# Moving the x projection of a four-direction selective scan into the in_proj and convolution stage

## Chip, cores and metric

The kernel runs on one core of one Trainium2 chip, as one launch. The metric is the device time of that launch in microseconds, as the median of several runs.

## What is computed

Four layers, one after the other, each on 4 images of 64 x 64 pixels with 192 channels. Cut to what matters here, one layer of the first three is:

```python
xn  = group_norm(x)                               # 192 channels
xc, z = split(xn @ in_proj.T)                     # 384 + 384 channels
u   = silu(depthwise_conv3x3(xc))                 # layers 1, 2, 3; layer 0 has u = xc
for k in range(4):                                # four scan directions over the 4096 pixels
    uk = order_k(u)                               # rows, columns, rows backwards, columns backwards
    dts, B, C = split(x_proj[k] @ uk)             # R + 16 + 16 rows; R = 12, 12, 96 in layers 0, 1, 2
    dt  = softplus(dt_w[k] @ dts + dt_bias[k])    # 384 channels
    h   = exp(dt * A) * h + dt * uk * B           # a scan over 4096 steps, 16 states a channel
    y  += back_k(sum_n(h * C) + D * uk)
x = x + out_proj(layer_norm(y) * gate(z))
```

Layer 3 has no scan: its convolution goes straight to the output stage. Everything is float32.

## The kernel before

The program loops over the images, and in each over the layers; a layer is up to three stages with a barrier of all engines behind each: `norm_conv`, `scan` (layers 0 to 2), `out_proj`. The 4096 pixels are cut into NCH = 8 chunks of T = 512, and the 384 inner channels into NDB = 3 blocks of 128 partitions. Orders of instructions inside a stage are written out by hand, per engine, and held together by semaphores.

**norm_conv** (L205 to L426). TensorE projects chunk by chunk (L403, 6 matmuls a chunk, two PSUM halves of 3 banks in turn), ScalarE normalises the next chunk's input (L356), VectorE copies the result out of PSUM: to `u` in layer 0, into the padded image `pad` otherwise (L305). Only when all 8 chunks are in `pad` does the convolution begin, as a second loop: 4 taps of 9 are matmuls with a diagonal matrix (L420), 5 taps are VectorE operations (L333, 15 a chunk), and ScalarE applies SiLU (L379). The last engine to finish ends the stage.

**scan** (L429 to L880). It opens with a preamble that projects direction k = 0 for all 8 chunks (L544 on TensorE, L755 on ScalarE, stores of `xd` and `b` to device memory on SyncE's queue, L507 and L456) and then loads the first chunk's inputs. The main part runs over 4 directions x 8 chunks x 3 blocks, 96 units a layer. A unit has 8 steps g of two states each. Per step TensorE multiplies dt*u by B through block-diagonal matrices (`inputs`, L583) and transposes weighted states to sum them (`sums`, L597), ScalarE makes the decays (L725) and keeps the last state (L714), VectorE scans (L828), GpSimd weighs with C (L868). Once a unit `make_dt` runs (L806, L811) on VectorE, at step g = 3 of the unit before, so the starts of L806 mark the units. In directions k = 0 to 2 the block d = 1 of each chunk also carries `project_x` for direction k + 1 of the same chunk (L544, one matmul at each of g = 5, 6, 7, into the bank that softplus uses):

```python
if d == 1 and g >= PE_XD and k + 1 < K:
    if g == PE_XD:
        pe.wait_ge(dt_made, unit(this, NDB - 1) + 1)
    project_x(k + 1, n, Z_BANK, g - PE_XD)
```

It reads `u` in the order of direction k + 1 (`in_order`, L167), which for odd directions is a column walk with a step of 64 floats. ScalarE takes the result out of PSUM (L781) and issues two stores (L785, L456). Direction k = 3 has nothing left to project.

The B rows of a chunk go from `b_dram` into a zeroed matrix in device memory, 4 bytes at a time, 4096 pieces to a DMA and two DMAs a chunk, on ScalarE's queue (`spread`, L708); from there they are loaded as `diag` (L487). The C rows are loaded broadcast to 128 partitions, four DMAs a chunk (`load_c`, L499), each of 4 rows that lie together in device memory.

Of the kernel before, what the change touches and what calls it, by code (L numbers as in the profile page):

```python
# [19 lines left out]
F32 = mybir.dt.float32  # L20
# [4 lines left out]
P = 128  # L25
IMAGES, H, W = 4, 64, 64
L = H * W
# [13 lines left out]
PE_LAG, PE_Z, PE_SKIP, PE_Y, PE_XD, PE_TR = 3, 1, 4, 5, 5, 6  # L41
ACT_B, ACT_XD, ACT_IN, ACT_LOG, ACT_YT, ACT_Y, ACT_TR = 4, 0, 2, 3, 3, 6, 7
# [4 lines left out]
PE_TAPS = 4  # L47
GN_EPS = 1e-5
LN_EPS = (1e-6, 1e-6, 1e-5, 1e-5)
RANK = (12, 12, 96)  # L50
MAX_LOG = 83.0
# [10 lines left out]
B_SCAN = (2 * RING + 4 + 2 + 1 + 2 + 1 + 3 + 1 + 1) * T  # L62
B_OUT = NCB * 2 * DI + NDB * DM + 2 * NDB * T + 2 * T + NCB * NCH * 6
# [9 lines left out]
def build(nc, x_in, ident_in, group_in, ones_in, w_in, w_out, w_xp, w_dt, vecs, out):  # L73
# [3 lines left out]
    with ctx:  # L77
# [18 lines left out]
        xp_w = sb("xp_w", [P, 2, NDB, P])  # L96
# [19 lines left out]
        xd_out = regB[:, o:o + T]; o += T  # L116
# [4 lines left out]
        xd_sb2 = dt  # L121
# [6 lines left out]
        tap_w = regB[:, o:o + PE_TAPS * NDB * P].rearrange("p (k d j) -> p k d j", k=PE_TAPS, d=NDB)  # L128
        xn = spare[0:CB, 0:2 * NCB * T].rearrange("p (q c t) -> p q c t", q=2, c=NCB)
        cv = spare[:, 2 * NCB * T:(2 * NCB + 2 * NDB) * T].rearrange("p (q d t) -> p q d t", q=2, d=NDB)  # L130
# [7 lines left out]
        x_stats = regB[0:CB, o:o + NCB * NCH * 6].rearrange("p (c n s) -> p c n s", c=NCB, n=NCH)  # L138
# [4 lines left out]
        xd_dram = [nc.dram_tensor(f"xd_{l}", (K, NCH, 1 + RANK[l] + 2 * NS, T), F32).ap() for l in range(3)]  # L143
# [4 lines left out]
        sems = [ctx.enter_context(nc.semaphore(f"s{i}")) for i in range(36)]  # L148
        all_sems = range(sems[0].num, sems[-1].num + 1)
        assert [s.num for s in sems] == list(all_sems)  # L150
# [51 lines left out]

        def norm_conv(l, b):
# [3 lines left out]
             cv_used, act_own, dve_own, a_made) = sems[:24]  # L207
            weights = 32 if last else 64

            XN_FREE, PAD_FREE = 2, 2  # L210
            CV_FREE = 2 * NDB
            DT_TAPS = TAPS - PE_TAPS
            STEP_FREE = CV_FREE * DT_TAPS

            with nc.Block(no_gpsimd_drain=True) as block:
                @block.sync
                def _(sp):
# [6 lines left out]
                    sp.dma_start(out_w, w_out[l]).then_inc(w_ready, 16)  # L224
                    if not last:
                        M = RANK[l] + 2 * NS
                        sp.dma_start(xp_w[:, :, :, 0:M], w_xp[l][:, 0:2]).then_inc(w_ready, 16)
                        sp.dma_start(dt_w[0:RANK[l] + 1], w_dt[l][:, 0:2]).then_inc(w_ready, 16)
                    if l in (1, 2):

                        sp.dma_start(x_dram, xT).then_inc(x_saved, 16)
                        sp.wait_ge(x_saved, 16)
# [4 lines left out]
                    sp.wait_ge(w_ready, weights)  # L237

                @block.gpsimd
                def _(pool):  # L240
                    if conv:
                        v = pad[:].rearrange("p d (h w) -> p d h w", w=PW)
# [3 lines left out]
                        nc.gpsimd.memset(v[:, :, 1:PW - 1, PW - 1], 0.0).then_inc(border, 1)  # L246

                @block.vector
                def _(dve):
                    dve.sem_inc(pad_made, PAD_FREE)  # L250
                    if conv:
                        dve.sem_inc(cv_step, STEP_FREE)

                    if l == 0:
                        for h, loaded in enumerate((x_half0, x_half1)):
                            dve.wait_ge(loaded, 16)
                            with dve.Fori(0, NCH // 2) as j:
                                chunk_stats(j + h * (NCH // 2), stats_made)
# [32 lines left out]

                    v = pad[:].rearrange("p d (h w) -> p d h w", w=PW)
                    if conv:
                        dve.wait_ge(border, 4)
                    with dve.Fori(0, NCH // 2) as j:
                        for q in range(2):
                            c = j * 2 + q
                            dve.wait_ge(in_mm, XN_FREE + c + 1)
# [937 lines left out]
```

## Time and profile before

| | |
|---|---|
| median of 3 runs | 30196.06 us (30186.81 to 30205.66) |
| the profiled execution: its own time, its span | 30209.58 us, 30207.7 us |
| PE, DVE, POOL, ACT busy, share of the span | 94%, 85%, 79%, 63% |
| TensorE clock granted, mean | 0.97 |
| device memory moved | 2545.53 MB read, 123.73 MB written, 88 GB/s |
| scan stages | 12 (3 layers x 4 images), 18432 scans, 1152 units |

The profile is of one execution. Shares are means over stages that differ much, so the stages are read one by one below. A layer's stages are told apart by the lines that open them: ScalarE's table load L340 opens norm_conv, L744 opens scan, L1001 opens out_proj.

### The profile page before, as it was taken

To read this page: it belongs to the slowest core of one execution; us is meant where nothing else is said; L and a number is where in the kernel's file an instruction comes from. 1 tells how busy PE (TensorE), PEld (TensorE's weight loads), DVE (VectorE), ACT (ScalarE), POOL (GpSimd) and SP (SyncE) were. 2 spreads that over 40 slices of the span, in tenths; PEclk is the share of its full clock that TensorE was granted. 3 is DMA by queue.
4 is the path that set the end of the run, shared out by engine and by line. 5 is a ranking of instruction groups with operands and counts; after the bars stand their busy time and mean duration, and the time that the engine had idled before them with its cause. 6 is when DMAs were issued, how large, how long until landed. Compare 5 with 4: busy or idle time off the path is not lost. (4 is left out here: it accounts for less than half of the span.)

```text
span 30207.7 us, 612992 instructions
## 1 busy us (share of the span) xinstructions
PE 28498.1 (94%) x244800; PEld 20286.3 (67%) x244800; DVE 25621.6 (85%) x23482; ACT 19104.5 (63%) x38088; POOL 23845.1 (79%) x10772
## 2 busy tenths in 40 slices
PE   9998998998999899899899989989989998998998
PEld 6775775774677577577467757757746775775774
DVE  7987996996798799699679879969968987996996
ACT  5665774774566577477466657747746665774774
POOL 7986995994798699599479869959947986995994
PEclk9999999999999999999999999999999999999999
DMA  3332332331333233233133323323313332332331
GB/s 100 100 95 71 102 103 67 106 108 43 97 101 94 71 102 102 69 105 109 42 97 100 94 71 102 103 69 105 109 43 97 102 91 74 102 101 69 106 107 43
DMA packets 3579914, 2695.33 MB, mean 89 GB/s; under 512 B 3269236, under 2 KB 3273548, under 8 KB 3323832
## 3 DMA queue, kind: packets, MB, share of 16 engines
q1 hardware_dynamic: 353272, 2592.36, 23.8%
q10 hardware_dynamic: 3223872, 64.57, 6.5%
q8 instruction: 1918, 31.42, 0.4%
q14 instruction: 852, 6.98, 0.1%
HBM read 2545.53 MB, written 123.73 MB: 88 GB/s over the span
## 5 line engine op out<-in xcount | busy, mean ns | idle before, releaser
L868 POOL TENSOR_TENSOR regB<-regB,regA 128x1024 f32<-128x1024 f32 x9216 | 21558.4, 2369 | 1760.6 <-ACT carry L714 1743.2
L828 DVE TENSOR_TENSOR_SCAN regB<-regB,carry,ps 128x512 f32<-128x512 f32 x16128 | 19217.5, 1259 | 1197.4 <-PE ps L583 1177.4
L725 ACT ACTIVATE regB<-regB,a_neg 128x512 f32<-128x512 f32 x18432 | 12225.6, 712 | 0.6
L583 PEld LDWEIGHTS ps<-regA,regB 64*128 64x128 f32 x147456 | 8992.5, 188 | 4164.4 <-issue 3185.4
L583 PE MATMUL ps<-regA,regB 64*128 64x128 f32 x147456 | 10739.4, 285 | 77.5 <-DVE regB L828 59.0
L597 PE MATMUL ps<-ident,regB 128*128 128x128 f32 x73728 | 10083.6, 280 | 184.3 <-POOL regB L868 125.2
L597 PEld LDWEIGHTS ps<-ident,regB 128*128 128x128 f32 x73728 | 7906.5, 141 | 1349.6 <-POOL regB L868 317.6
L714 ACT ACTIVATE carry<-regB 128x2 f32<-128x2 f32 x9216 | 1900.2, 206 | 5949.7 <-DVE regB L828 5358.8
L858 POOL TENSOR_TENSOR regB<-regB,u 128x512 f32<-128x512 f32 x1152 | 1630.5, 1415 | 2142.0 <-DVE regB L811 2142.0
L828 DVE TENSOR_TENSOR_SCAN regB<-regB,ps 128x512 f32<-128x512 f32 x2304 | 2624.5, 1201 | 375.1 <-PE ps L583 341.4
L544 PE MATMUL ps<-u,xp_w 128*44 128x512 f32 (+3 forms) x2304 | 1678.7, 834 | 158.4 <-ACT L744 114.0
L1139 POOL TENSOR_TENSOR regB<-regB 128x512 f32<-128x512 f32 x128 | 187.0, 1461 | 2006.8 <-ACT regB L1026 2006.6
L614 PE MATMUL ps<-pad,ident 128*128 128x512 f32 x1728 | 1376.4, 883 | 8.2 <-ACT regB L734 8.2
L558 PE MATMUL ps<-regB,dt_w 13*128 13x512 f32 (+1 forms) x2304 | 1268.6, 631 | 78.7 <-DMA regB<-xd 78.7
L806 DVE SCALAR_TENSOR_TENSOR ps<-regB,ps 128x512 f32<-128x512 f32 x1152 | 776.9, 674 | 477.5 <-ACT regB L684 477.5
L692 ACT ACTIVATE regB<-ps 128x512 f32<-128x512 f32 x1152 | 671.4, 583 | 746.6 <-PE ps L565 746.3
L420 PE MATMUL ps<-pad,regB 128*128 x2304 | 1012.9, 602 | 30.1 <-DVE pad L305 30.1
L740 ACT ACTIVATE pad<-ps 128x512 f32<-128x512 f32 x1152 | 943.9, 819 | 38.9 <-PE ps L620 38.9
L927 PE MATMUL ps<-regA,regB 96*128 96x512 f32 x1536 | 702.7, 621 | 272.1 <-ACT regA L983 272.1
L565 PEld LDWEIGHTS ps<-ident,regB 128*128 128x128 f32 x4608 | 537.8, 143 | 474.8 <-issue 391.9
L420 PEld LDWEIGHTS ps<-pad,regB 128*128 128x128 f32 x2304 | 442.5, 193 | 600.4 <-issue 600.4
L675 ACT ACTIVATE regB<-ps 128x512 f32<-128x512 f32 x1152 | 681.2, 591 | 240.1 <-PE ps L558 223.1
(81 smaller groups left out, 14465.4 us busy)
## 6 DMA issues: line engine op xcount, KB each, us to landing
regA<-xd SPq DMA_DIRECT2D x1536, 1024.0 KB, 4.7
regA<-eye SPq DMA_DIRECT2D x384, 2048.0 KB, 7.7
regA<-x_in SPq DMA_DIRECT2D x16, 1536.0 KB, 14.4
x_keep<-regA SPq DMA_DIRECT2D x8, 3072.0 KB, 18.8
regA<-x_keep SPq DMA_DIRECT2D x16, 1536.0 KB, 15.9
regB<-xd SPq DMA_DIRECT2D x128, 192.0 KB
xd<-regB ACTq DMA_DIRECT2D x96, 256.0 KB
xd<-regB ACTq DMA_DIRECT2D x192, 88.0 KB
```

What stands on the lines that cost most here:

```text
L420: last_mm = nc.tensor.matmul(ps[:, 3 * q + d, :].rearrange("p (r w) -> p r w", w=W), tap_w[:, tap, d, :], v[:, d, bass.ds(c * RW + tap // ...
L544: mm = nc.tensor.matmul(as_chunk(ps[0:M, bank, :], k), xp_w[:, k % 2, d, 0:M], in_order(u, k, d, n), start=d == 0, stop=d == NDB - 1)
L558: nc.tensor.matmul(ps[:, Z_BANK, :], dt_w[0:R + 1, k % 2, d * P:(d + 1) * P], dts[0:R + 1], start=True, stop=True).then_inc(z_mm, 1)
L583: mm = nc.tensor.matmul(b.rearrange("p (t s) -> p s t", s=2), dtuT[at, up, q, :], diag[at, cp, q, g], start=True, stop=True)
L597: mm = nc.tensor.matmul(ps[:, Y_BANK + up, at], ring[:, g % RING, s, at], ident[:], start=g == 0 and s == 0 and q == 0, stop=g == PAIRS - ...
L614: nc.tensor.matmul(as_chunk(ps[:, Y_BANK + up, :], k), w, in_order(src, k, d, n), start=True, stop=False)
L714: nc.scalar.activation(carry[:, d, 2 * g:2 * g + 2], ring[:, g % RING, :, T - 1 if c[0] < 2 else 0], ACT.Copy).then_inc(carried, 1)
L725: nc.scalar.activation(decays[:, g % 2, s], dt[:, up, :], ACT.Exp, scale=a_neg[:, c[0], d, 2 * g + s:2 * g + s + 1]).then_inc(a_made, 1)
L740: nc.scalar.activation(in_order(y_acc, k, d, n), as_chunk(ps[:, Y_BANK + up, :], k), ACT.Copy).then_inc(y_kept, 1)
L828: nc.vector.tensor_tensor_scan(ring[:, g % RING, s, way], decays[:, g % 2, s, way], b[:, s, way], 0.0 if begun else carry[:, d, at:at + 1] ...
L858: nc.gpsimd.tensor_tensor(dtu.rearrange("p (q i r) -> p i q r", i=ROWS, q=QS), dt[:, up, :].rearrange("p (i q r) -> p i q r", i=ROWS, q=QS ...
L868: nc.gpsimd.tensor_tensor(ring[:, g % RING], ring[:, g % RING], c_all[:, g], ALU.mult).then_inc(g_made, 1)
```

## The change

`norm_conv` becomes one pipeline over chunks, written out without hardware loops, that also makes the x projection of all four directions; `scan` loses both the preamble and `project_x`.

- The projection is made in plain pixel order from the chunk of `u` just made. In layers 0 and 1 two directions share one matmul of 2 x 44 output rows (`PASSES`), so a chunk has 2 passes of 3 matmuls; in layer 2 (128 rows a direction) 4 passes of 3.
- Device memory holds `xd` as whole rows of 4096 pixels in the order of the direction's walk (`xd_dram`, now K x rows x L). The even directions (0, 2) are stored by SyncE as pieces of 512 pixels. For the odd directions (1, 3) ScalarE writes its PSUM copy transposed to (w, h) order, 8 pixels of a column together, and issues the stores itself: every piece is 8 floats, 32 bytes. Nothing in `norm_conv` waits for the last of these; `scan` waits for them before direction 1.
- With a transposed copy, B and C rows of chunk n in a backwards direction are those of chunk 7 - n (`place`).
- The number of taps on TensorE is 0, 2, 1, 3 in layers 0 to 3 (before 4 everywhere); VectorE has the other 7, 8 and 6 in layers 1 to 3.
- `pad` is filled by ScalarE instead of VectorE (`fill_pad`), `out_w` is no longer loaded in `norm_conv` of layers 0 to 2, and the store of x to `x_keep` is waited for late.
- The first chunk's `dts`, `diag` and C rows are loaded at the end of `norm_conv`, by SyncE behind `store_even(6)`.
- C rows now lie 16 KB apart, so a load of 4 rows reads 2 KB pieces where it read 8 KB.

```diff
-PE_TAPS = 4
+PE_TAPS = (0, 2, 1, 3)
+PASSES = (((0, 2), (1, 3)), ((0, 2), (1, 3)), ((0,), (2,), (1,), (3,)))
...
-        xd_dram = [nc.dram_tensor(f"xd_{l}", (K, NCH, 1 + RANK[l] + 2 * NS, T), F32).ap() for l in range(3)]
+        xd_dram = [nc.dram_tensor(f"xd_{l}", (K, 1 + RANK[l] + 2 * NS, L), F32).ap() for l in range(3)]
...
+                    store_even(0)
+                    store_even(1)
+                    sp.wait_ge(even_stored[0], EVEN)
+                    sp.wait_ge(ones_set, 1)
+                    sp.dma_start(dts[0:RANK[l]], dts_rows(l, 0, 0)).then_inc(dts_loaded, 16)
+                    spread_rows(sp, l, 0, 0, 0, spread_b)
+                    for c in range(2, NCH):
+                        store_even(c)
+                        if c == NCH - 2:
...
+                            sp.dma_start(diag[:, 0].rearrange("p q g t -> p (q g t)"),
+                                         eye_dram[0, 0:P * EYE].rearrange("(p x) -> p x", p=P)).then_inc(diag_loaded, 16)
+                            sp.wait_ge(in_mm, NCH)
+                            for h in range(PAIRS // 2):
+                                sp.dma_start(c_all[:, 2 * h:2 * h + 2], c_rows(l, 0, 0, h).partition_broadcast(P)
+                                             ).then_inc(c_loaded, 16)
...
+                    def keep_x(c):
...
+                        for i, ks in enumerate(passes):
+                            n, rows = c * NP + i, len(ks) * M
+                            odd = i >= NP // 2
+                            act.wait_ge(xd_mm, n + 1)
...
+                            if odd:
+                                wait(act, odd_stored[c % 2], c // 2 * odd_each(l))
+                            else:
+                                wait(act, even_stored[c % 2], c // 2 * EVEN)
+                            dst, src = staged(i, c)[0:rows], ps[0:rows, 6 + n % 2, :]
+                            if odd:
+                                dst = dst.rearrange("p (w h) -> p h w", h=RW)
+                                src = src.rearrange("p (h w) -> p h w", w=W)
+                            nc.scalar.activation(dst, src, ACT.Copy).then_inc(xd_copied, 1)
...
+                                for part in odd_parts(l):
+                                    act.dma_start(to[part], rows[part]).then_inc(odd_stored[c % 2], 16)
+                                to = b_dram[l][k].rearrange("c (a n r) -> n (c a) r", n=NS, r=H)[:, :, c * RW:(c + 1) * RW]
+                                act.dma_start(to, rows[RANK[l]:RANK[l] + NS]).then_inc(odd_stored[c % 2], 16)
...
+                    for c in range(NCH + 1):
+                        if c:
+                            silu(c - 1)
+                        if c + 4 < NCH:
+                            normalise(c + 4)
+                        if c + 3 < NCH:
+                            fill_pad(c + 3)
+                        if c:
+                            keep_x(c - 1)
...
+                    for c in range(NCH + 1):
+                        if c + 1 < NCH:
+                            taps(c + 1)
+                        if c + 3 < NCH:
+                            project_in(c + 3)
+                        if c:
+                            project_x(c - 1)
...
-                                if d == 1 and g >= PE_XD and k + 1 < K:
-
-                                    if g == PE_XD:
-                                        pe.wait_ge(dt_made, unit(this, NDB - 1) + 1)
-                                    project_x(k + 1, n, Z_BANK, g - PE_XD)
```

**TensorE in the scan**, block d = 1 of a chunk in direction 0, before (L583 is `inputs`, L597 `sums`, L620 `turn_y`, L565 `turn_dtu`, L544 `project_x`):

```order
L583 MATMUL ps<-regA,regB 128x2x64 x8
L597 MATMUL ps<-ident,regB 128x128 x8
L620 MATMUL ps<-ident,regB 128x128 x4
L544 MATMUL ps<-u,xp_w 44x512
L583 MATMUL ps<-regA,regB 128x2x64 x8
L597 MATMUL ps<-ident,regB 128x128 x8
L544 MATMUL ps<-u,xp_w 44x512
L565 MATMUL ps<-ident,regB 128x128 x4
L583 MATMUL ps<-regA,regB 128x2x64 x8
L597 MATMUL ps<-ident,regB 128x128 x8
L544 MATMUL ps<-u,xp_w 44x512
```

and the same place after (L711, L725, L748, L693 in that order of names):

```order
L711 MATMUL ps<-regA,regB 128x2x64 x8
L725 MATMUL ps<-ident,regB 128x128 x8
L748 MATMUL ps<-ident,regB 128x128 x4
L711 MATMUL ps<-regA,regB 128x2x64 x8
L725 MATMUL ps<-ident,regB 128x128 x8
L693 MATMUL ps<-ident,regB 128x128 x4
L711 MATMUL ps<-regA,regB 128x2x64 x8
L725 MATMUL ps<-ident,regB 128x128 x8
```

The three projection matmuls are gone and nothing stands in their place.

**ScalarE in norm_conv of layer 2**, one chunk in the middle, after (L437 `silu`, L423 `normalise`, L429 `fill_pad`, L456 the copies of `keep_x`, L465 and L467 its stores; the last numbers of a DMA's shape are pieces and floats a piece):

```order
L437 ACTIVATE u<-regB,vec 128x512 x3
L423 ACTIVATE regA<-regA,gn_bias,gn_rstd 96x512 x2
L429 ACTIVATE pad<-ps 128x3x8x64
L456 ACTIVATE regB<-ps 128x512 x2
L456 ACTIVATE xd_odd<-ps 128x8x64 x2
L465 DMA xd<-xd_odd 3072x1x8 x2
L465 DMA xd<-xd_odd 1024x1x8
L467 DMA b<-xd_odd 16x64x8
L465 DMA xd<-xd_odd 3072x1x8 x2
L465 DMA xd<-xd_odd 1024x1x8
L467 DMA b<-xd_odd 16x64x8
```

Before, this loop held L379 alone; now each chunk issues 8 DMAs of 16384 pieces in all from this engine's queue (in layers 0 and 1 there are 6 DMAs of 5632 pieces).

## Rows read from the trace of the kernel before

**Rows 1.** The page, busy time by engine over the span.
```profile
PE 28498.1 (94%) x244800; PEld 20286.3 (67%) x244800; DVE 25621.6 (85%) x23482; ACT 19104.5 (63%) x38088; POOL 23845.1 (79%) x10772
```

**Rows 2.** Busy time by stretch: directions 0 to 2 and 3, layers 1 and 2.
```profile
core 0: us, PE busy (x) PEld busy (x) DVE busy (x) ACT busy (x) POOL busy (x), PEclk, DMA share, GB/s
10114.10:11684.60 1570.50, 1552.39 (x14722) 1160.92 (x14723) 1441.69 (x1289) 1085.38 (x2243) 1427.61 (x643) 1.00 0.35 101
11684.60:12156.90 472.30, 471.56 (x4695) 369.23 (x4694) 463.23 (x416) 351.05 (x713) 463.57 (x208) 1.00 0.35 104
12557.90:14120.50 1562.60, 1530.35 (x14721) 1172.46 (x14722) 1442.41 (x1288) 1084.09 (x2242) 1427.72 (x643) 0.99 0.36 107
14120.50:14589.20 468.70, 467.40 (x4695) 368.69 (x4694) 463.25 (x416) 349.90 (x713) 463.04 (x208) 1.00 0.36 107
```

**Rows 3.** Waits of DVE in one scan of layer 1 (total us, times, longest).
```profile
DVE regB L828 <- PE ps L583: 134.5, 160, 5.3
```

**Rows 4.** Timeline of DVE, `make_dt` alone: start, us; directions 0, then 1.
```profile
10547.10 0.68 DVE L806 SCALAR_TENSOR_TENSOR ps<-regB,ps 128x512 f32<-128x512 f32 x1
10572.42 0.67 DVE L806 SCALAR_TENSOR_TENSOR ps<-regB,ps 128x512 f32<-128x512 f32 x1
10592.49 0.67 DVE L806 SCALAR_TENSOR_TENSOR ps<-regB,ps 128x512 f32<-128x512 f32 x1
...
10742.96 0.68 DVE L806 SCALAR_TENSOR_TENSOR ps<-regB,ps 128x512 f32<-128x512 f32 x1
10766.62 0.67 DVE L806 SCALAR_TENSOR_TENSOR ps<-regB,ps 128x512 f32<-128x512 f32 x1
10787.18 0.68 DVE L806 SCALAR_TENSOR_TENSOR ps<-regB,ps 128x512 f32<-128x512 f32 x1
```

**Rows 5.** Timeline of PE in that scan, direction 0, `project_x` and its neighbour.
```profile
10554.87 1.89 PE L544 MATMUL ps<-u,xp_w 128*44 128x512 f32 x2
10556.69 0.66 PE L565 MATMUL ps<-ident,regB 128*128 128x128 f32 x4
```

**Rows 6.** Busy time from the start of norm_conv to the first scan, layers 0 to 3 (layer 3: to out_proj).
```profile
7563.60:7684.60 121.00, 74.67 (x174) 29.34 (x176) 27.47 (x39) 26.19 (x41) 1.26 (x1) 0.77 0.33 83
9926.80:10120.90 194.10, 158.44 (x366) 66.27 (x368) 98.14 (x143) 47.47 (x78) 2.44 (x5) 0.89 0.17 52
12364.20:12564.60 200.40, 162.58 (x366) 71.29 (x368) 98.03 (x142) 47.50 (x78) 2.41 (x5) 0.88 0.21 62
14797.10:14944.70 147.60, 129.50 (x292) 56.74 (x292) 96.11 (x138) 35.12 (x57) 1.10 (x4) 0.93 0.03 7
```

**Rows 7.** Timeline of PE: first in_proj matmuls of layer 0; taps of layer 1 (two records are one matmul).
```profile
7591.50 18.79 PE L403 MATMUL ps<-regA,regB 96*128 96x512 f32 x38 [2.67 <-ACT regA L356]
...
9994.58 21.62 PE L420 MATMUL ps<-pad,regB 128*128 x50
```

**Rows 8.** L333 alone over the convolution of layer 1: us, DVE busy (x), PEclk, DMA share, GB/s.
```profile
9984.20:10071.80 87.60, 80.26 (x120) 0.97 0.00 0
```

**Rows 9.** Timeline of the start of scan, layer 1.
```profile
10073.58 1.28 ACT L744 ACT_TABLE_LOAD   x1 [0.91 <-PEq L426]
...
10114.15 0.70 DVE L806 SCALAR_TENSOR_TENSOR ps<-regB,ps 128x512 f32<-128x512 f32 x1 [39.90 <-ACT regB L684]
...
10120.89 1.22 DVE L828 TENSOR_TENSOR_SCAN regB<-regB,ps 128x512 f32<-128x512 f32 x1 [5.32 <-PE ps L583]
```

**Rows 10.** Costs of ScalarE's pieces, by form (busy us, mean ns, idle before).
```profile
L379 ACT ACTIVATE u<-regA,vec 128x512 f32 x288 | 196.7, 724 | 1004.9 <-DVE regA L333 1004.9
...
L995 ACT ACTIVATE u<-ps 128x1536 f32<-128x1536 f32 x48 | 69.7, 1452 | 179.5 <-PE ps L927 179.5
```

**Rows 11.** Timeline of ACT and its sequencer in the scan: the two DMAs of `spread`.
```profile
10524.37 0.54 ACTq L708 DMA_DIRECT2D eye<-b  x1
...
10524.94 3.15 ACTq L708 DMA_DIRECT2D eye<-b  x1
```

**Rows 12.** The page, DMA queue of ScalarE (packets, MB, share of 16 engines); issues with KB each, us to landing.
```profile
q10 hardware_dynamic: 3223872, 64.57, 6.5%
...
regA<-xd SPq DMA_DIRECT2D x1536, 1024.0 KB, 4.7
regA<-eye SPq DMA_DIRECT2D x384, 2048.0 KB, 7.7
...
eye<-b ACTq DMA_DIRECT2D x768, 16.0 KB, 11.2
```

More of the change, by code:

```diff
@@ L256, in _ @@
                             dve.wait_ge(loaded, 16)
-                            with dve.Fori(0, NCH // 2) as j:
+                            for j in range(NCH // 2):
                                 chunk_stats(j + h * (NCH // 2), stats_made)
@@ L363, in _ @@
                     if not conv:
+                        normalise(2)
+                        for c in range(NCH):
+                            if c + 3 < NCH:
+                                normalise(c + 3)
+                            keep_x(c)
                         return
@@ L366, in _ @@
                     act.wait_ge(w_ready, weights)
-                    for tap in range(PE_TAPS):
+                    for tap in range(PT):
                         for d in range(NDB):
@@ new lines, in _ @@
+                    fill_pad(0)
+                    normalise(2)
+                    fill_pad(1)
+                    normalise(3)
+                    fill_pad(2)
+                    for c in range(NCH + 1):
[7 more added lines that the diff above has]
+                            keep_x(c - 1)
@@ new lines, in taps @@
+                    def taps(c):
+                        pe.wait_ge(pad_made, min(c + 2, NCH))
+                        for d in range(NDB):
+                            if c:
+                                pe.wait_ge(cv_step, step_of(c - 1, 0, d))
+                            for tap in range(PT):
+                                mm = nc.tensor.matmul(
+                                    ps[:, d, :].rearrange("p (r w) -> p r w", w=W), tap_w[:, tap, d, :],
+                                    v[:, d, c * RW + tap // 3:c * RW + tap // 3 + RW, tap % 3:tap % 3 + W],
+                                    start=tap == 0, stop=tap == PT - 1)
+                            mm.then_inc(cv_mm, 1)
@@ new lines, in project_x @@
+                    def project_x(c):
+                        if last:
+                            return
+                        ready_u(pe, c)
+                        for i, ks in enumerate(passes):
+                            n, rows = c * NP + i, len(ks) * M
+                            wait(pe, xd_copied, n - 1)
+                            for d in range(NDB):
+                                w = (i * NDB + d) * rows
+                                mm = nc.tensor.matmul(ps[0:rows, 6 + n % 2, :], xp_w[:, w:w + rows],
+                                                      u[:, d, c * T:(c + 1) * T], start=d == 0, stop=d == NDB - 1)
+                            mm.then_inc(xd_mm, 1)
@@ L407, in _ @@
+                    project_in(1)
+                    if not last:
+                        pe.wait_ge(xw_loaded, 16)
                     if not conv:
+                        for c in range(NCH):
+                            if c + 2 < NCH:
+                                project_in(c + 2)
+                            project_x(c)
                         return
-                    v = pad[:].rearrange("p d (h w) -> p d h w", w=PW)
-                    pe.wait_ge(tap_made, PE_TAPS * NDB)
+                    pe.wait_ge(tap_made, PT * NDB)
```

355 lines of the change are left out of this document (171 added, 184 removed).

## Prediction

> **What bounds the kernel now.** I read the busy shares first [rows 1]. TensorE is busy 94% of the span and VectorE 85%, so either could set the pace, and a mean over stages cannot say which. The next view is busy time by stretch, with the borders put on the directions of one scan [rows 2]. Directions 0 to 2 of layer 1 take 1570.5 us and direction 3 takes 472.3 us, from the first `make_dt` of a direction to that of the next, and for direction 3 to its last one. That is 72 units at 21.81 us against 23 intervals at 20.53 us. The only work that direction 3 lacks is `project_x` with its copy and stores, so the kernel holds its own comparison: a unit with nothing to project is 1.28 us shorter on average. In the same stretches PE is busy 1552 of 1570 us and 471.6 of 472.3 us. VectorE waits for TensorE's L583 134.5 us in one scan [rows 3]. The scan is bound by TensorE, with VectorE and GpSimd just behind: in direction 3 they are busy 463 us each of 472.
>
> The timeline of `make_dt` shows where it goes [rows 4]. In direction 0 the interval that holds `project_x` lasts 10572.42 - 10547.10 = 25.32 us, and the one behind it 20.07 us. In direction 1 they are 23.66 and 20.56 us. So one chunk's projection costs 5.25 us where it reads columns (for directions 1 and 3) and 3.10 us where it reads rows (for direction 2). The PE timeline agrees with the first: one L544 matmul to its successor is 1.82 us [rows 5], three are 5.5. A tap matmul, read in rows, takes 21.62 / 25 = 0.865 us [rows 7].
>
> Then the stages between the scans [rows 6]: from the start of norm_conv to the first scan 121.0, 194.1 and 200.4 us in layers 0, 1, 2, and 147.6 us for layer 3 up to out_proj. VectorE is busy in half of that, since the convolution only starts when in_proj has ended and the scan's preamble comes behind both.
>
> **What leaves the scan.** `project_x`, 24 chunks a scan. In layers 0 and 1: 16 x 5.25 + 8 x 3.10 = 108.8 us, if the freed interval falls to that of its neighbour [rows 4]. The other way to count is to give every unit direction 3's interval: 1570.5 - 72 x 20.53 = 92 us [rows 2]. I take the first, because even directions show 20.07 us where TensorE has nothing extra, and keep the second as the low end. For layer 2 I take the same count by blocks: 1562.6 - 72 x 20.38 = 95 us. Per image 2 x 108.8 + 95 = 313 us (low end 279). VectorE is late next, and `spread` still holds ScalarE once a chunk. The C loads now read 2 KB pieces. They land 4.7 us after issue now [rows 12] and are wanted about six steps of 2.5 us later, so I cost them at nothing; that cover of some 10 us would have to be used up.
>
> **The preamble.** From scan's table load to the first `make_dt` is 40.6 us and from there to the first scan 6.7 us [rows 9]. The first shrinks to table load, three small scalings and four softplus steps, about 5.4 us by the same timeline. So 12 us stay of 47.
>
> **The norm_conv stages.** Their length now comes from the slowest engine of one pipeline.
>
> Layer 0: TensorE starts 27.9 us in [rows 6, 7] and has 8 x (6 + 6) matmuls: 96 x 0.865 = 83 us, up from 42. Behind it hang the loads of `diag` and C, issued some 5 us before TensorE ends; alone they take 7.7 + 4 x 4.7 = 26.5 us in a row [rows 12], overlapped less. I take 15 us exposed (ends 8 and 21). With a barrier: 127.5 + 12 = 139.6 us against 121.0, so **+19**.
>
> Layer 1: start-up about 22 us (two projected chunks, 10.4; two pad copies of 1.45 [rows 10]; first taps). Then per chunk TensorE has 18 matmuls, 15.6 us, and VectorE 21 tap operations at 87.6 / 120 = 0.73 us [rows 8], 15.3 us: 8 x 15.6 = 125. Tail: last SiLU 0.7, last x projection 5.2, copies, store issues and barrier 6. Sum 159 + 12 = 171 against 194.1: **-23**.
>
> Layer 3: 24 + 144 x 0.73 + 2.5 = 131.6 against 147.6: **-16**.
>
> Layer 2 turns on a cost that the trace shows only from afar. Its TensorE needs 21 matmuls a chunk, 18.2 us, and VectorE 17.5 us. But ScalarE's queue must also take 16384 pieces of 32 bytes per chunk. The nearest rows are the two `spread` DMAs of 4096 pieces of 4 bytes: the second one's issue holds ScalarE's sequencer for 3.15 us [rows 11], and what ScalarE has next stands behind it. They land 11.2 us after issue [rows 12]. The low end per piece is the busy time of the DMA engines: 6.5% of 30207 us on 16 engines over 3.22 million packets is 9.7 ns an engine, 0.61 ns a piece. The high end is one DMA alone, 11.2 us / 4096 = 2.7 ns. I take the pair, 11.2 / 8192 = 1.37 ns, since a long row of DMAs is most like a pair. Then a chunk's stores take 22.4 us, more than the 18.2 of TensorE, and with ScalarE held in their issue, `silu`, `normalise` and `fill_pad` of later chunks queue behind: the stage runs at the pace of the stores. First batch at 52 us, eight of 22.4, less 7.5 still in flight when ScalarE is let go, barrier and 12: 238 against 200.4, **+37**. At the low end the stage is TensorE's, 22 + 145 + 26 + 12 = 206, or +6. In layers 0 and 1 a chunk has 5632 pieces, 7.7 us, below the 10.4 and 15.6 us of TensorE: hidden, so long as a piece stays under 1.8 ns in layer 0.
>
> The trace shows 4-byte pieces leaving an engine every 9.7 ns [rows 12]. The Trainium skill's page "DMA: Bandwidth & Descriptors", section Specifications, says that transfers under 512 B make the DMA engine read, modify and write. If that doubled the engine's 9.7 ns it would be 1.2 ns a piece and 29,000 us in all, so rule and row part only if the penalty is several times larger, which is the fourth case below.
>
> **Sum.** Per image -313 + 19 - 23 + 37 - 16 = -296 us; four images -1184 us. On the profiled execution, 30209.6 us, that gives 29,025; the median of the runs is 13.5 us lower, so 29,010 us.
>
> **Other ways it could go.** (a) The stores cost 0.6 to 1.1 ns a piece: layer 2 costs +6, the sum is -328 an image, time 28,880. For it: 256 pieces an engine need only 2.5 us of its time. Against it: ScalarE visibly stands in L708.
> (b) The gain is smaller: scan intervals fall only to direction 3's 20.53 us and a piece costs 2 ns, so layer 2 is +120 and layer 0 +21: -279 + 21 - 23 + 120 - 16 = -177 an image, 29,490 us; with one of the two alone about 29,200 to 29,350. At 2.7 ns it would be 29,900.
> (c) The stores flood: each odd piece, written with a step of 256 bytes, is so dear that ScalarE's queue sets all three stages. At r ns a piece the three take, against now, 131 r - 142, 45 r - 143 and 45 r - 69 us; with -16 and -313 the sum is 221 r - 683 us an image. It decides from r = 3.1 ns, or 50 ns an engine; at 4 ns the time is 31,000. For it: each piece is a partial write, and no row shows 32 bytes to a strided place. Against it: L708 writes smaller ones to places as scattered at 1.37 ns.
> (d) The change does not do what it says: VectorE is the real bound, `project_x` was covered, and the scan stays at 2043 us. Then only the stages move, +17 an image, 30,265. The difference of 25.32 to 20.07 us in neighbouring units speaks against it [rows 4].
>
> **Chances.** Forecast 0.55, (a) 0.22, (b) 0.15, (c) 0.05, (d) 0.03. Within 0.2% (60 us, about what a measurement of this kernel can tell) has hardly a case of its own: 0.02, out of the edges of (b) and (d). Slower 0.06, faster 0.92. The range is 28,800 to 29,450: below, (a) with somewhat more won at the stages' tails; above, (b) without its worst corner.
>
> **What would show it.** Right: no interval between two `make_dt` over 21 us in steady chunks, even directions near 20.1, scans of 1930 to 1950 us from first to last `make_dt`; 12 us from scan's table load to the first scan; norm_conv of layer 2 with ScalarE's sequencer in L465 most of the time and chunks of about 22 us, layer 1's at 15.6. Wrong: chunks of layer 2 at 18 us or over 30; intervals near 20.5 in even directions; VectorE waiting for C loads at the start of chunks.

## Result and the profile after

The change made the kernel slower: 32007.41 us (median of 4 runs, 31997.39 to 32021.70) against 30191.44 us (4 runs, 30181.60 to 30205.66), a ratio of 1.060 with a 95% interval of 1.058 to 1.062. The forecast was 29,010 us with a range of 28,800 to 29,450. The profiled execution has a span of 31995.7 us.

From the page of the kernel after: busy time by engine, two of the costliest groups with the idle time ahead of them, DMA queues, and DMA issues with the median time to landing.

```profile
PE 27893.6 (87%) x242880; PEld 20718.7 (65%) x242880; DVE 25798.2 (81%) x23950; ACT 19104.5 (60%) x37984; POOL 23811.1 (74%) x10784
...
q1 hardware_dynamic: 1049336, 2606.52, 36.9%
q10 hardware_dynamic: 3953792, 40.59, 7.5%
...
L953 POOL TENSOR_TENSOR regB<-regB,regA 128x1024 f32<-128x1024 f32 x9216 | 21519.6, 2376 | 2908.7 <-ACT carry L820 2900.0
L914 DVE TENSOR_TENSOR_SCAN regB<-regB,carry,ps 128x512 f32<-128x512 f32 x16128 | 19186.7, 1258 | 2259.0 <-ACT regB L831 1528.1
...
regA<-xd SPq DMA_DIRECT2D x1536, 1024.0 KB, 11.1
regA<-eye SPq DMA_DIRECT2D x384, 2048.0 KB, 7.8
```

No engine is fuller than before [rows 1]: all four lose share, so the added time is waiting. Both large groups now wait for ScalarE. For GpSimd that is an old wait that has grown, for VectorE a new one; the same two groups on the page of the kernel before:

```profile
L868 POOL TENSOR_TENSOR regB<-regB,regA 128x1024 f32<-128x1024 f32 x9216 | 21558.4, 2369 | 1760.6 <-ACT carry L714 1743.2
L828 DVE TENSOR_TENSOR_SCAN regB<-regB,carry,ps 128x512 f32<-128x512 f32 x16128 | 19217.5, 1259 | 1197.4 <-PE ps L583 1177.4
```

And the C loads (`regA<-xd`) land 11.1 us after issue (the median) where they took 4.7 [rows 12], while the `diag` load beside them is nearly unchanged (7.8 against 7.7). Of queue q1 the 1,049,336 packets take 36.9% of the span. These loads overlap one another, so the rate of one can't be had by dividing 1 MB by its time to landing: over the four loads of one chunk 143 GB/s are moved, with the DMA engines busy for 0.85 of the time.

```profile
10882.60:10912.20 29.60, 26.61 (x274) 21.39 (x274) 25.53 (x24) 16.32 (x35) 22.22 (x11) 1.00 0.85 143
```

Busy time by stretch, the columns of [rows 2]: from norm_conv's start to the first scan in layers 0, 1, 2 (layer 3: to out_proj), then directions 0 to 2 and direction 3 of layer 1.

```profile
8000.30:8169.80 169.50, 93.32 (x220) 38.60 (x222) 27.05 (x37) 34.13 (x49) 1.79 (x2) 0.76 0.56 83
10482.30:10698.80 216.50, 144.14 (x318) 58.45 (x320) 115.33 (x182) 64.34 (x88) 2.87 (x6) 0.82 0.40 65
13035.80:13342.20 306.40, 174.64 (x366) 75.17 (x368) 131.20 (x205) 76.70 (x101) 2.91 (x6) 0.77 0.46 67
15688.20:15830.80 142.60, 110.52 (x244) 47.23 (x244) 98.45 (x154) 44.04 (x62) 1.18 (x4) 0.91 0.03 7
10692.00:12311.00 1619.00, 1484.15 (x14578) 1188.41 (x14579) 1437.99 (x1288) 1067.92 (x2218) 1423.89 (x643) 0.96 0.49 93
12311.00:12829.90 518.90, 488.95 (x4693) 384.64 (x4692) 464.41 (x415) 348.22 (x713) 463.92 (x208) 0.95 0.50 95
```

TensorE's busy time in directions 0 to 2 fell by 68 us, and the stretch still grew from 1570.5 to 1619.0. Direction 3, whose work the change does not touch, grew from 472.3 to 518.9 us. That alone says that something beside the removed projection was added to every chunk. TensorE's granted clock, 1.00 in both before, is 0.96 and 0.95 here, where it is idle between its matmuls for 134.9 of 1619.0 and 30.0 of 518.9 us.

All stages of image 1 (the second of four), in us; a scan is taken from its first `make_dt` to its last (the time from there to the first scan stays at 6.7), and the last rows are experiments told below:

| | to first scan, L0 / L1 / L2 | L3 | scans, L0 / L1 / L2 | kernel |
|---|---|---|---|---|
| before | 120.9 / 194.1 / 200.4 | 147.6 | 2044.0 / 2042.7 / 2031.3 | 30191 |
| forecast | 139.6 / 171 / 238 | 131.6 | 1935 / 1934 / 1936 | 29010 |
| after | 169.5 / 216.5 / 306.4 | 142.6 | 2112.5 / 2137.9 / 2147.5 | 32007 |
| e3, rows 18 KB apart | 147.2 / 202.6 / 285.6 | 142.7 | 1934.0 / 1938.5 / 1933.7 | 29443 |
| e5, and SyncE stores | 148.4 / 177.1 / 214.0 | 142.5 | 1939.0 / 1934.8 / 1937.9 | 29067 |
| e9, and late first loads | 131.8 / 165.4 / 198.8 | 142.2 | 1941.4 / 1939.6 / 1935.5 | 28901 |
| e10, after with late spread | 170.8 / 223.1 / 308.9 | 142.5 | 1984.7 / 1991.5 / 1967.3 | 30229 |
| e11, e9 with late spread | 133.0 / 165.6 / 199.3 | 144.2 | 1979.7 / 1981.3 / 1957.6 | 29347 |

Against the forecast, an image is 592 us longer in its scans and 155 us in its stages, 747 in all, and four such images make up 2,990 of the 2,997 us of the miss.

**Inside a chunk.** The timeline of VectorE, `make_dt` alone (start, us), direction 0 of layer 1:

```profile
10884.36 0.68 DVE L892 SCALAR_TENSOR_TENSOR ps<-regB,ps 128x512 f32<-128x512 f32 x1
10904.44 0.67 DVE L892 SCALAR_TENSOR_TENSOR ps<-regB,ps 128x512 f32<-128x512 f32 x1
10932.33 0.67 DVE L892 SCALAR_TENSOR_TENSOR ps<-regB,ps 128x512 f32<-128x512 f32 x1
10952.40 0.68 DVE L892 SCALAR_TENSOR_TENSOR ps<-regB,ps 128x512 f32<-128x512 f32 x1
```

Two intervals of three are 20.07 and 20.08 us, what a unit without projection took before [rows 4]; the third is 27.89. In it lie these rows of ScalarE (ACTq is its sequencer) and of SyncE's sequencer:

```profile
10902.23 0.52 ACTq L226 DMA_DIRECT2D eye<-b  x1
...
10902.78 9.65 ACTq L226 DMA_DIRECT2D eye<-b  x1
...
10912.48 0.20 ACT L820 ACTIVATE carry<-regB 128x2 f32<-128x2 f32 x1 [8.25 <-issue]
```

```profile
10882.63 15.95 SPq L646 DMA_DIRECT2D regA<-xd  x4
```

The four C loads are issued between 10882.6 and 10898.6, and the last of them, issued at 10898.22, takes 14.0 us and lands at 10912.2; `spread` (L226) comes at 10902, and its second DMA holds ScalarE's sequencer for 9.65 us where it took 3.15 [rows 11]. `keep_last` (L820) and the decays (L831) stand behind it. GpSimd waits for L820 as well:

```profile
10912.82 2.35 POOL L953 TENSOR_TENSOR regB<-regB,regA 128x1024 f32<-128x1024 f32 x1 [7.31 <-ACT carry L820]
```

Over the whole scan of layer 1, ScalarE's waits in the kernel after (us in total, times, longest): once a chunk, 31 times, it stands still for an issue, 245 us together.

```profile
ACT carry L820 <- issue: 244.9, 31, 10.8
```

The same row of the kernel before:

```profile
ACT carry L714 <- issue: 52.5, 28, 2.7
```

The difference, 192 us, is nearly the 204 by which that scan exceeds its forecast. SyncE's loads are not themselves awaited: no wait of GpSimd for `regA<-xd` stands among its waits there, and none of TensorE for `diag`.

The hold of 9.65 us ends at 10912.4, 0.3 us behind the landing of the last C load. It is so in nearly every chunk: over the 30 chunks of that scan it ends 0.9 us after the last landing (the median; four in five between 0.5 and 1.9 us). What holds the sequencer lasts as long as the C loads do.

**The steady part and the end of norm_conv.** ScalarE's timeline in layer 2, `silu` (L437) and the issue of the odd stores (L465, L467), in the steady part and at the end:

```profile
13198.82 1.95 ACT L437 ACTIVATE u<-regB,vec 128x512 f32<-128x512 f32 x3 [10.23 <-issue]
...
13212.88 4.84 ACTq L465 DMA_DIRECT2D xd<-xd_odd  x3
13217.76 0.67 ACTq L467 DMA_DIRECT2D b<-xd_odd  x1
13218.47 5.06 ACTq L465 DMA_DIRECT2D xd<-xd_odd  x3
13223.56 0.67 ACTq L467 DMA_DIRECT2D b<-xd_odd  x1
13224.28 1.95 ACT L437 ACTIVATE u<-regB,vec 128x512 f32<-128x512 f32 x3 [10.30 <-issue]
...
13266.11 31.17 ACTq L465 DMA_DIRECT2D xd<-xd_odd  x3
```

A chunk takes 25.5 to 26.9 us in this ring: `silu` 2, TensorE's x projection of that chunk 12 to 13.5 (10.5 in the first chunk, where the granted clock is 1.00; here it is 0.78 to 0.88), the last copy, which runs beside the first store's issue, 11.3 us of issue, and then the next `silu`, which stands behind the issue in ScalarE's queue. Near the end the same L465 takes 31.17 us instead of about 5: SyncE has just issued the next stage's `diag` and C loads,

```profile
13263.49 0.38 SPq L327 DMA_DIRECT2D regA<-eye  x1
13263.91 6.97 SPq L331 DMA_DIRECT2D regA<-xd  x4
```

and the last chunk's `silu`, projection and stores all wait. In layers 0 and 1 the pair of L465 in the same place holds ScalarE 26.65 and 20.83 us, against 1.5 to 2.3 us in other chunks.

### The profile page after: what moved, and what is told of

It reads as the page before. It is cut to its first block and busy times, and to the rows that moved or that the text cites. A ratio compares the mean times of both kernels' runs of the same rounds, so it can differ in the third digit from the quotient of the medians.

```text
span 31995.7 us, 601560 instructions
## 1 busy us (share of the span) xinstructions
PE 27893.6 (87%) x242880; PEld 20718.7 (65%) x242880; DVE 25798.2 (81%) x23950; ACT 19104.5 (60%) x37984; POOL 23811.1 (74%) x10784
## 3 DMA queue, kind: packets, MB, share of 16 engines
q1 hardware_dynamic: 1049336, 2606.52, 36.9%
## 5 line engine op out<-in xcount | busy, mean ns | idle before, releaser
L831 ACT ACTIVATE regB<-regB,a_neg 128x512 f32<-128x512 f32 x18432 | 12184.5, 710 | 0.6
L725 PE MATMUL ps<-ident,regB 128*128 128x128 f32 x73728 | 10406.8, 286 | 1844.3 <-POOL regB L953 1830.2
L711 PEld LDWEIGHTS ps<-regA,regB 64*128 64x128 f32 x147456 | 9212.7, 192 | 3602.0 <-issue 2917.1
L711 PE MATMUL ps<-regA,regB 64*128 64x128 f32 x147456 | 10974.3, 289 | 115.1 <-DVE regB L914 71.0
L725 PEld LDWEIGHTS ps<-ident,regB 128*128 128x128 f32 x73728 | 8174.6, 144 | 3019.3 <-POOL regB L953 1955.2
L820 ACT ACTIVATE carry<-regB 128x2 f32<-128x2 f32 x9216 | 1884.7, 204 | 8309.9 <-DVE regB L914 5405.3
L550 PE MATMUL ps<-u,regB 128*88 128x512 f32 (+1 forms) x1536 | 779.6, 667 | 620.9 <-ACT u L437 613.9
L414 DVE SCALAR_TENSOR_TENSOR regB<-pad,vec,regB 128x512 f32<-128x512 f32 x1728 | 1152.8, 745 | 0.0
L550 PEld LDWEIGHTS ps<-u,regB 128*88 128x88 f32 (+1 forms) x1536 | 297.4, 197 | 1094.9 <-ACT u L437 653.9
L693 PE MATMUL ps<-ident,regB 128*128 128x128 f32 x4608 | 862.7, 320 | 83.2 <-POOL regB L943 82.9
L804 ACT ACTIVATE regB<-ps 128x512 f32<-128x512 f32 x1152 | 671.9, 583 | 302.8 <-PE ps L693 302.7
L897 DVE TENSOR_TENSOR regB<-ps,regB 128x512 f32<-128x512 f32 x1152 | 796.8, 692 | 39.5
## 6 DMA issues: line engine op xcount, KB each, us to landing
regA<-xd SPq DMA_DIRECT2D x1536, 1024.0 KB, 11.1
```

What stands on the lines that cost most here:

```text
L414: nc.vector.scalar_tensor_tensor(dst, src, wt, part, ALU.mult, ALU.add).then_inc(cv_step, 1)
L550: mm = nc.tensor.matmul(ps[0:rows, 6 + n % 2, :], xp_w[:, w:w + rows], u[:, d, c * T:(c + 1) * T], start=d == 0, stop=d == NDB - 1)
L711: mm = nc.tensor.matmul(b.rearrange("p (t s) -> p s t", s=2), dtuT[at, up, q, :], diag[at, cp, q, g], start=True, stop=True)
L725: mm = nc.tensor.matmul(ps[:, Y_BANK + up, at], ring[:, g % RING, s, at], ident[:], start=g == 0 and s == 0 and q == 0, stop=g == PAIRS - ...
L820: nc.scalar.activation(carry[:, d, 2 * g:2 * g + 2], ring[:, g % RING, :, T - 1 if c[0] < 2 else 0], ACT.Copy).then_inc(carried, 1)
L831: nc.scalar.activation(decays[:, g % 2, s], dt[:, up, :], ACT.Exp, scale=a_neg[:, c[0], d, 2 * g + s:2 * g + s + 1]).then_inc(a_made, 1)
```

## Experiments

Each runs beside the kernel before on the same chip, which took 30272.62 us in the first group (e1 to e4), 30250.59 in the second (e5 to e8) and 30257.52 in the third (e9 to e11); with the change itself it took 30191.44. So a difference between runs of two groups can be some 80 us off, and where it is small the stage times in the table bear it out. Where no interval is given, the time is of one run.

**e1: the kernel before with rows 16 KB apart.** One line of layout and its reader; nothing is moved.

```diff
-        xd_dram = [nc.dram_tensor(f"xd_{l}", (K, NCH, 1 + RANK[l] + 2 * NS, T), F32).ap() for l in range(3)]
+        xd_dram = [nc.dram_tensor(f"xd_{l}", (K, 1 + RANK[l] + 2 * NS, L), F32).ap() for l in range(3)]
```

> The kernel before with one part of the change alone: xd in device memory as rows of 4096 pixels, so that the four C rows of a load are 2 KB pieces 16 KB apart instead of 8 KB in one piece. Theory A (the C loads are what stretches the scan: 2 KB pieces take the DMA engines 177 ns each, a load lands after 11 us instead of 4.7, and ScalarE's issue of the spread DMAs is held behind them): every chunk's first full unit grows by 6 to 8 us, a scan by 170 to 210 us, the kernel comes out near 32,300 to 32,700 us, with C loads landing after 10 to 11 us. Rival B (the stretch of the scan comes from something else in the changed kernel, such as where the small stores put the B rows): about 30,200 us, C loads at 4.7 us.

Measured: 32640.11 us, 2,367 more than before. Its page (C loads) and its ACT timeline:

```profile
regA<-xd SPq DMA_DIRECT2D x1536, 1024.0 KB, 10.9
```

```profile
10930.01 11.91 ACTq L708 DMA_DIRECT2D eye<-b  x1
```

The layout alone makes the slow loads, the long hold, and scans of 2224 to 2258 us. The miss of the forecast's scans, 4 x 592 = 2,368 us, is about as large.

**e2: the kernel before with pieces of 2 KB, rows 2,112 bytes apart.** It tells the size of the pieces from the distance of the rows.

```diff
-(K, NCH, 1 + RANK[l] + 2 * NS, T), F32).ap()
+(K, NCH, 1 + RANK[l] + 2 * NS, T + 16), F32).ap()[:, :, :, 0:T]
```

> The kernel before with its C rows kept close together but 64 bytes apart from each other, so that a load still reads 2 KB pieces, now at a pitch of 2112 bytes. If the size of the pieces is what costs (theory A1): as with rows 16 KB apart, 32,300 to 32,700 us, C loads landing after 10 to 11 us. If the pitch of 16 KB is what costs (A2): 30,200 us, loads at 4.7 to 5.5 us, a 2 KB piece at 90 ns.

Measured: 30254.49 us, within 0.1% of before; loads land after 5.6 us. Four times as many pieces are worth 0.9 us of landing and nothing of time. So the distance of the rows is the cause, and not the size of the pieces.

**e3: the change with rows 18 KB apart.** The same rows and pieces, 2 KB of padding behind each row.

```diff
-(K, 1 + RANK[l] + 2 * NS, L), F32).ap()
+(K, 1 + RANK[l] + 2 * NS, L + 512), F32).ap()[:, :, 0:L]
```

> The changed kernel with rows of xd 18 KB apart instead of 16 KB, nothing else. A1 (size): stays at 32,000 us. A2 (pitch of a power of two): the scan loses its stretch of 170 to 205 us, three scans and four images, and the ends of norm_conv some 20 us each: about 29,450 us.

Measured: 29443.39 us, 2,564 less than the change, 2.7% under the kernel before. Page and ACT timeline:

```profile
regA<-xd SPq DMA_DIRECT2D x1536, 1024.0 KB, 4.8
```

```profile
10905.46 3.41 ACTq L226 DMA_DIRECT2D eye<-b  x1
```

Over the four C loads of a chunk 158 GB/s are moved with the DMA engines busy for 0.51 of the time, against 143 at 0.85 in the change:

```profile
10885.00:10912.00 27.00, 26.93 (x280) 21.82 (x278) 26.54 (x26) 19.13 (x41) 26.10 (x13) 1.00 0.51 158
```

The scans are the forecast's within 5 us each. Of the 2,997 us of the miss this is 86%. The same 1,049,336 packets of queue q1 now take 25.6% of 29,442 us, 7,537 us for each of the 16 DMA engines against 11,806 in the change.

**e4: the change with the C rows of a chunk copied together in device memory** (one more small copy a chunk on SyncE, loads of 8 KB pieces from it).

```diff
+        c_dram = [nc.dram_tensor(f"c_{l}", (K, NCH, NS * T), F32).ap() for l in range(3)]
...
+            eng.dma_start(c_dram[l][k, n].rearrange("(m t) -> m t", t=T),
+                          xd_dram[l][k][o:o + NS, at * T:(at + 1) * T]).then_inc(sem, 16)
```

> The changed kernel with the 16 C rows of each chunk first copied inside device memory into 32 KB in one piece (one small DMA more a chunk, on SyncE's queue), and loaded from there in 8 KB pieces. Both A1 and A2: C loads land after about 4.7 us again, intervals of make_dt go to 20.1 and 20.6 us (the unit with the spread DMAs to 20.5), scans of 1930 to 1950 us instead of 2112 to 2145, ScalarE's issue of a spread DMA is held 3 us instead of 10, the 20 to 30 us for which it is held at the end of norm_conv shrink below 10: about 29,450 us. If the stretch has another cause: stays over 31,500 us.

Measured: 29553.28 us, scans 1938 to 1943, C loads 4.7 us. A second way to be rid of the stride gives the same scans; the stages are 7 us longer than in e3 in layer 0 and 9 in layer 2, with the copies in them.

**e6: the change with rows 16,448 bytes apart.** As e3 with `L + 16`.

> The changed kernel with rows of xd 64 bytes further apart (16448 bytes instead of 16384). If it is the exact power of two that makes the four rows of a load meet in the same part of the memory, and any offset spreads them: as with 18 KB, 29,450 us and C loads after 4.8 us. If the pieces must be kilobytes away from the same place: C loads stay at 8 to 11 us and the time above 31,000 us.

Measured: 31863.13 us; C loads 11.1 us, scans 2115 to 2141. Rows 64 bytes further apart load as slowly as in the change; 2 KB further apart they load quickly.

The Trainium skill's page "DMA: Bandwidth & Descriptors", section "Latency and other measured facts", says that large row distances at powers of two slow copies of 128 rows (207 GB/s at 512 KiB, 164 at 2 MiB, 103 at 4 MiB), that 4 KiB of padding restores the rate and 192 bytes don't. The runs agree in the shape of it: slow at 16 KB and 64 bytes beside it, quick with 2 KB of padding (e1, e6, e3; 10.9, 11.1 and 4.8 us to landing). They differ in the distance at which it begins: here it is 16 KB already, in a load of four rows read by 128 partitions.

**e10: the change as it is, with `spread` issued some 15 us later,** when the slow loads have landed. It tells the slow loads from the queue behind them.

```diff
-                                if d == 0 and after and g == ACT_B:
+                                if d == 1 and after and g == 2:
                                     spread(after, 1 - par)
```

> The change as it is, rows 16 KB apart, but ScalarE issues the spread of the next chunk's B rows in block d = 1, step 2, instead of block d = 0, step 4, some 15 us later, when the slow C loads have landed. Theory (ScalarE's queue is held behind the C loads, and that is what the scan loses): the hold of the second L226 falls from 9.65 us to about 3, C loads still land some 11 us after issue, and a scan takes 1940 to 1960 us from first to last make_dt instead of 2112 to 2148; total 29,650 to 29,850 us. Rival (the C rows themselves come late for GpSimd, or the traffic slows what runs beside it): a scan stays over 2050 us and the total over 31,000.

Measured: 30229.12 us (10 runs), ratio 0.999 (0.998 to 1.000). From its page, its ACT timeline, its waits of ACT and those of POOL in the scan of layer 1:

```profile
regA<-xd SPq DMA_DIRECT2D x1536, 1024.0 KB, 11.4
```

```profile
10923.57 2.81 ACTq L226 DMA_DIRECT2D eye<-b  x1
```

```profile
ACT carry L820 <- issue: 22.9, 7, 4.5
```

```profile
POOL regB L953 <- ACT carry L820: 100.9, 69, 6.7
POOL regB L953 <- DMA regA<-xd: 1.3, 2, 0.9
```

The loads are as slow as ever and GpSimd waits 1.3 us for them in a scan, but the long hold is gone and with it 1,778 us. The mechanism of the theory held. Its numbers did not: the scans, 1967 to 1992 us, all missed its 1940 to 1960, and the total missed its 29,650 to 29,850 by 379 us. e11 looks for the reason.

**e11: e9 with the same late spread,** to see what the new place costs by itself.

> The version with rows 18 KB apart, SyncE's odd stores and late first loads, and with the spread in block d = 1, step 2. The C loads are quick here, so the remaining hold of about 3.2 us a chunk should vanish only if it comes from the C loads. Theory of the queue: at most 1 us a chunk is gained, 96 chunks x 3 layers over 4 images, so between no difference and 380 us less than the same version without it. Rival (the hold of the second spread is that of its own 4096 pieces, as in the kernel before): the same time within 0.2%.

Measured: 29346.59 us (5 runs), ratio 0.970 (0.969 to 0.971), 445 us slower than e9. Both expectations missed: no gain came, and the time is 1.5% longer. In block d = 1 the two DMAs hold ScalarE just ahead of `make_dt` (VectorE waits 1.59 us for a decay there in the stretch read): the interval in which they are issued and the next take 20.6 to 21.5 us (medians) where e9 has 20.1 to 21.2. So the place costs 22 us a scan in layer 2 and some 40 in layers 0 and 1. The hold of the second DMA stays at 2.8 to 2.9 us (medians of the three layers), away from any C load, so about as much as in the kernel before is the spread's own, as the rival had it. It also closes e10's account: e10's scans are 5, 10 and 10 us longer than e11's. That is all that slow C loads cost a scan once nothing queues behind them, against the 179 to 214 us a scan by which the change exceeds e3.

**e7: e3 with the first `diag` and C loads at the scan's start again.**

```diff
-                            sp.dma_start(diag[:, 0].rearrange("p q g t -> p (q g t)"),
-                                         eye_dram[0, 0:P * EYE].rearrange("(p x) -> p x", p=P)).then_inc(diag_loaded, 16)
...
+                    load_diag(chunk_of(0, 0, 0), 0)
+                    for h in range(PAIRS // 2):
+                        load_c(chunk_of(0, 0, 0), h)
```

> Rows 18 KB apart, and the first chunk's diag and C rows loaded at the start of scan as before, not behind store_even(6) in norm_conv. If the loads at the end of norm_conv hold ScalarE's issue of the small stores and so the last chunk's silu (theory C): the issues of chunk 6 take 4 to 5 us in layers 0 and 1 and 10 us in layer 2 instead of 14 to 23, norm_conv is 12 to 15 us shorter, and scan pays 10 to 15 us more before its first scan: within 100 us of 29,443. If the hold has another cause, norm_conv stays as long and the time is 120 to 180 us above 29,443.

Measured: 29278.39 us, 165 less than e3. The stages are 14.7, 16.0 and 11.9 us shorter to the first scan, which still follows the table load by 11.3 us. I had expected the scan to pay 10 to 15 us for it, and it pays nothing: the loads had cover at the scan's start, and bringing them forward cost time.

**e5: e3 with all odd stores on SyncE's queue.**

```diff
-                                    act.dma_start(to[part], rows[part]).then_inc(odd_stored[c % 2], 16)
+                                    sp.dma_start(to[part], rows[part]).then_inc(odd_stored[c % 2], 16)
```

> Rows of xd 18 KB apart, and the stores of the odd directions issued by SyncE instead of ScalarE. Theory C (in layer 2 ScalarE walks a ring: silu 2 us, then it waits about 8.5 us for the x projection that this silu releases, copies, then stands 10 us in the issues of the stores before the next silu, 25 us a chunk; at the end of every norm_conv it stands behind the loads of diag and C): without the issues the ring falls away, layer 2 is TensorE's with 18 us a chunk, and nothing stands behind the loads but SyncE. From the start of norm_conv to the first scan: layer 2 about 200 us instead of 286, layer 1 about 170 instead of 193 to 203, layer 0 about 135 instead of 147; the scans unchanged at 1934 to 1940 us. In all 29,443 - 4 x 125 = 28,950 us. Rival D (the DMA engines cannot take the small pieces faster, so the buffers of two chunks hold ScalarE instead): layer 2 stays above 260 us and the time above 29,350 us.

Measured: 29067.23 us (4 runs), ratio 0.961 (0.959 to 0.962), 376 less than e3. Layer 2 loses 71.6 us and layer 1 25.5: the ring through ScalarE is gone. The total is 117 us over the 28,950 expected. Its SP timeline shows what is left, the stores of chunk 7 behind the next stage's loads:

```profile
12057.96 1.02 SPq L343 DMA_DIRECT2D regA<-eye  x1
12059.03 6.23 SPq L347 DMA_DIRECT2D regA<-xd  x4
...
12070.33 9.92 SPq L322 DMA_DIRECT2D xd<-xd_odd  x3
```

**e8: e5's stores without the padding.** As e5, on rows 16 KB apart.

> The changed kernel with its rows 16 KB apart and the odd stores on SyncE's queue. The two costs should add if they are separate: the stages between scans as in the run with both edits except that the loads of C at the end of norm_conv last some 25 us (layer 0 up by 10 to 15 us), and the scans stretched as in the changed kernel, 2112 to 2145 us; in all about 31,400 to 31,500 us.

Measured: 31654.13 us, 353 less than the change. The gain of the stores' move is nearly the same with slow and quick C loads (376), so the two add; it was 150 to 250 us less than I expected. The scans stay at 2117 to 2149, which also shows that who stored the rows does not matter to them.

**e9: padding, SyncE's stores and late first loads together.**

> The change with rows 18 KB apart, all odd stores issued by SyncE, and the first diag and C loads back at the start of the scan, so that no store of chunk 7 stands behind them. Theory (SyncE's queue at the end of norm_conv cost layers 1 and 2 of the version with SyncE's stores some 12 and 20 us): from norm_conv's table load to the scan's table load about 120 us in layer 0, 152 in layer 1, 182 in layer 2 (against 137, 166, 202), scans unchanged at 1935 to 1940 us from first to last make_dt; 49 us an image less than 29067, so about 28,870 us. Rival (SyncE's own 11 us of issue for the stores of chunk 7 end the stage whatever stands ahead of them): layer 2 stays at 195 or more, and the time is 28,950 or above.

Measured: 28901.24 us (5 runs), ratio 0.955 (0.954 to 0.956), the best of all, 9.7% under the change. The scan's table load comes 120.5, 154.1 and 187.5 us after norm_conv's, where 120, 152 and 182 were expected. In the first half of layer 2's stage a chunk takes 18.0 us, TensorE's pace; when in_proj has ended the x projections come 13.4 us apart, and SyncE ends the stage at 14.2 us a chunk, 11.3 of it stores of 32-byte pieces:

```profile
11937.22 4.83 SPq L322 DMA_DIRECT2D xd<-xd_odd  x3
...
11951.42 4.79 SPq L322 DMA_DIRECT2D xd<-xd_odd  x3
```

## Why the prediction was wrong

**The step that failed** is the sentence on the C loads in the part on what leaves the scan: "They land 4.7 us after issue now and are wanted about six steps of 2.5 us later, so I cost them at nothing; that cover of some 10 us would have to be used up." It fell in two places. The duration of the old layout was carried to the new one, though the four rows of a load had moved from 2 KB to 16 KB apart; it became 11.1 us. And I asked who waits for the loads, and not what is queued while they are in flight. The cover did hold: GpSimd never waits for C to speak of. But `spread` on ScalarE's queue stands behind them, and ScalarE's program behind `spread`: the hold of about 9 us a chunk is what the term put at nothing should have carried, 179 to 214 us a scan against e3. e10 separates the two: 1,778 of the 2,564 us that padding gives back come back by moving `spread` alone, and some 445 more would, if its new place costs there what it costs in e11. Most of the rest is the ends of norm_conv, 67 us an image shorter in e3 than in e10. I had even noted that `spread` holds ScalarE once a chunk, and left it at its old size.

**The x projection out of the scan: right.** Intervals of 20.07 and 20.56 us are the ones forecast, and 1934 to 1939 us in e3 the scans: 312 us an image are won there, where 313 were forecast. The higher of my two counts was the right one.

**The preamble: right.** 11.3 us from table load to first scan, 12 forecast.

**Layer 0, +19 forecast, +49 measured.** Of the 15 us taken for the loads at the end I had only the loads' own time. They also held ScalarE's stores for 26.65 us. Without them (e9) it is +11.

**Layer 1, -23 forecast, +22 measured.** The same hold, 14 us of it by the padding (e3) and 16 by the late loads (e7); 21 more are the stores in ScalarE's program, which e9 has not. e9 gives -29, and its x projections follow each other at 15.5 us while in_proj runs, TensorE's pace as forecast (15.6), and at 8.2 to 10.3 behind it.

**Layer 2, +37 forecast, +106 measured.** The price of a piece was taken too high, 1.37 ns; 16384 pieces hold a sequencer 11.3 us, which is 0.69 ns, near my low end of 0.61. But the same low price gave 25.5 us a chunk, not the 18.2 of case (a), because I let issue and TensorE run side by side. They are in one ring, through `silu` behind the stores, and add. With the stores on SyncE and the first loads late (e9) the stage falls just below its old length (198.8 against 200.4).

**Layer 3, -16 forecast, -5 measured:** a small term, not looked into.

**The rivals.** None named this. (c) put the slow side on the stores and needed 3.1 ns a piece; the time came out slower at 0.69 ns, by another queue. (a) had the price of a piece right. (b) is refuted by the intervals of 20.07 us and the 0.69 ns, (d) by e3. The list of what would show the forecast wrong had "VectorE waiting for C loads at the start of chunks", one engine and one wait away from what happened. The paragraph on small transfers has a slip: at 1.2 ns a piece my own sum gives 28,920 us and not 29,000. And e3's 29,443 us, at the very edge of my range, is no support for the stage terms: they are 7, 32, 48 and 11 us an image too low there, and only the scans are right.

**What stays open.** Why rows 16 KB apart take so much longer to read; the runs show the distance, not the cause. That the hold of `spread` goes with the C loads ahead of it is shown by where it ends, by e3 and by e10. By what means a load on SyncE's queue holds ScalarE's sequencer is not shown; a run with other traffic in place of the C loads was not made.

## What to carry to other kernels

When a layout changes, price each of its readers anew by the distance between the rows it reads together; 2 KB of padding behind each 16 KB row, one line, was worth 2,564 us here. A load that nobody waits for can still cost its full length: look at which engine issues a DMA while it is in flight, and what that engine has to do next. And here many small pieces were better off on the queue of an engine that has nothing to compute (376 us, e5), with the next stage's loads behind them and not ahead (166 us more, e9).

## What the runs showed of the hardware

- A broadcast load of four 2 KB rows to 128 partitions (1 MB) lands 4.8 us after issue with rows 18 KB apart, 5.6 us at 2,112 bytes, 11.1 us at 16 KB and 11.1 us at 16 KB + 64 bytes.
- Of a pair of DMAs of 4096 pieces of 4 bytes each, the first holds the issuing sequencer 0.52 us and the second about 3 (3.15, 3.41 and 2.81 us in the kernel before, e3 and e10); just behind such slow loads of another engine's queue the second took 9.65 us (the change) and 11.91 (e1), until about when the last of the loads had landed. Three store issues of 5 us together took 31.17 behind `diag` and four of them.
- Pieces of 32 bytes, written to scattered places, hold the sequencer 0.69 ns each, 16384 of them 11.3 us, on ScalarE's queue and on SyncE's alike; that is half of what the landing of the pair of `spread` DMAs had led me to [rows 12].
